# Sandwich block on one core: inverse roots of the feed-forward part's norms made on GpSimd by a bit guess and three Newton steps

## The reference

```
_layernorm(x) = (x - mean(x)) / sqrt(var(x) + 1e-5)        # over the last axis, 128
x = x + _layernorm(attention(_layernorm(x)))               # 16 heads of 8, relative bias, causal
x = x + _layernorm(ffn(_layernorm(x)))
ffn(x): h = silu(x @ w1.T * s1) * (x @ w2.T * s2)          # 128 -> 512
        h = gelu(h @ h1.T * sh1)                           # 512 -> 512
        h = gelu(h @ h2.T * sh2)                           # 512 -> 512
        return h @ w3.T * s3                               # 512 -> 128
```

## Time and profile before

| what | us |
|---|---|
| median of 3 runs | 781.52 |
| the profiled execution, whole | 783.46 |
| its span, first to last instruction | 781.7 |
| feed-forward stage, from the first matmul of layer 0 to the end | about 570 to 781.7 |
| ScalarE table loads at the roots of `stage3` (L1716, L1720) | 8 of 1.283 |
| `Sqrt` of `rs` in `stage3`, each | 0.208 |

### The profile page before, as it was taken

How to read it: one execution, slowest core, us unless ns; L and a number is a source line. 1 busy time by engine, 2 the same in 40 slices (tenths; PEclk the granted TensorE clock), 3 DMA queues, 4 the chain that set the end, 5 groups by cost and what they waited for, 6 DMA issues and landing times. The chain is left out here.

```text
span 781.7 us, 19102 instructions
## 1 busy us (share of the span) xinstructions
PE 648.1 (83%) x8066; PEld 471.8 (60%) x8066; DVE 551.1 (70%) x928; ACT 557.1 (71%) x654; POOL 273.9 (35%) x185
## 2 busy tenths in 40 slices
PE   4527743499999999999999999997779899898993
PEld 2213313367667667676676766764568688687682
DVE  3829983277777778778787777876665757768546
ACT  1445542389798798988989889887657867778663
POOL 2213341806309045090450813601062181441801
PEclk9777875589999999999999999998989999999998
DMA  3471376122314214123142231404020000000001
GB/s 72 114 268 56 100 216 188 18 62 58 101 32 95 64 52 114 55 75 83 44 114 63 66 93 35 123 29 136 14 81 2 0 1 1 1 27 2 1 27 55
DMA packets 40143, 53.53 MB, mean 68 GB/s; under 512 B 5664, under 2 KB 30528, under 8 KB 37632
## 3 DMA queue, kind: packets, MB, share of 16 engines
q1 hardware_dynamic: 40056, 52.28, 24.6%
HBM read 39.59 MB, written 11.94 MB: 66 GB/s over the span
## 5 line engine op out<-in xcount | busy, mean ns | idle before, releaser
L961 PE MATMUL p_s<-q_sb,k_sb 96*128 96x128 bf16 (+1 forms) x1600 | 171.0, 249 | 18.3 <-DVE probs L1107 14.5
L1225 ACT ACTIVATE probs<-p_s 128x1024 f32<-128x1024 f32 x160 | 156.6, 1017 | 18.2 <-DVE p_s L1116 10.6
L1225 ACT ACTIVATE probs<-probs 128x1024 f32<-128x1024 f32 x128 | 133.5, 1055 | 46.4 <-DVE probs L1107 46.2
L1005 PE MATMUL p_o<-probs,v_sb 128*32 128x128 f32 (+1 forms) x3200 | 159.8, 331 | 7.5 <-ACT o_acc L1243 4.7
L961 PEld LDWEIGHTS p_s<-q_sb,k_sb 96*128 96x128 bf16 x1600 | 113.0, 100 | 77.6 <-issue 29.4
L917 POOL TENSOR_SCALAR_AFFINE_SELECT even_b<-even_b 128x2048 f32<-128x2048 f32 x32 | 75.4, 2357 | 220.2 <-ACT even_b L1236 220.2
L1107 DVE TENSOR_TENSOR probs<-p_s,even_b 128x1024 f32<-128x1024 f32 x96 | 115.0, 1220 | 27.5 <-PE p_s L961 15.4
L1005 PEld LDWEIGHTS p_o<-probs,v_sb 128*32 128x32 f32 x3200 | 84.6, 111 | 40.7 <-issue 13.5
L1654 PE MATMUL p_z<-hid_hi,h_hi 128*128 128x512 f32 x256 | 102.0, 398 | 1.7 <-POOL hid_lo L1575 1.7
L1657 PE MATMUL p_z<-hid_lo,h_hi 128*128 128x512 f32 x256 | 101.0, 395 | 0.0
L982 PE MATMUL p_s<-q_rows,rel_w 72*128 72x64 bf16 x2048 | 84.8, 197 | 18.2 <-DVE probs L1107 8.7
(11 more groups left out here) (177 smaller groups left out, 883.7 us busy)
## 6 DMA issues: line engine op xcount, KB each, us to landing
k_sb<-k_dram SPq DMA_DIRECT2D x48, 192.0 KB
q_sb<-q_dram SPq DMA_DIRECT2D x16, 576.0 KB
q_rows<-qr_dram SPq DMA_DIRECT2D x42, 192.0 KB
q_dram<-q_parts SPq DMA_DIRECT2D x12, 256.0 KB, 6.1
k_dram<-k_parts SPq DMA_DIRECT2D x12, 256.0 KB, 6.1
qr_dram<-q_turned SPq DMA_DIRECT2D x12, 256.0 KB, 6.1
x_all<-in_L_attn_x_dram SPq DMA_DIRECT2D x4, 512.0 KB, 4.7
every<-in_L_ffn_h_w_dram SPq DMA_DIRECT2D x2, 1024.0 KB, 8.2
```

Of the source, the lines that this page charges most:

```text
L961: last = nc.tensor.matmul(slot[:, c:c + n * BLK], k_sb[hg][:, h * S + j * BLK:h * S + (j + 1) * BLK], ap(q_sb[hg], at, [[HG * S, KROWS], [ ...
L1005: last = nc.tensor.matmul(p_o[32 * h:32 * h + 32, at:at + blocks * BLK], v_sb[hg][:, j, h * 32:(h + 1) * 32], probs[n % PBUFS][:, h, col * ...
L1225: nc.scalar.activation(to, got, ACT.Exp, scale=SCALE).then_inc(t_exp, 1)
```

## The change

In `stage3` the roots go from ScalarE to GpSimd. There `inverse_root` makes 1 / sqrt(x) of the 128 by 8 tile in 13 instructions (`ROOT_OPS`), each of which waits for the one before: a first guess from the bits (one), and then three Newton steps of four. Two columns of the statistics tile (`st3` or `st4`, stride of 6 elements) are its working space, and the result is in column 1. VectorE's reciprocals in `stage3` go as well. GpSimd's order becomes: `pre_root(n+1, 0)`, `gather(n+2)`, `add_x(n+1)`, `post_root(n-1)`, `pre_root(n+1, 1)`, the splits, `add_x1(n-1)`, and at the end `post_root(3)`. The norms of batch 0 in the attention stage keep `Sqrt` and reciprocal.

```diff
--- before.py
+++ after.py
@@ -86,6 +86,9 @@
 NZ = 4
 HC = HID // 128
 PRE, POST = 12, 5
+ROOT_GUESS = 0x5F3759DF
+ROOT_STEPS = 3
+ROOT_OPS = 1 + 4 * ROOT_STEPS
 
 
 class First:
@@ -127,9 +130,33 @@
     nc.vector.tensor_scalar(rs[:, :], mv[:, :, 1], EPS, None, ALU.add).then_inc(chain, 1)
 
 
+def inverse_root(nc, pool, x, room, done, at):
+
+    bits = mybir.dt.int32
+    t, y = room[:, :, 0], room[:, :, 1]
+    nc.gpsimd.tensor_scalar(y.bitcast(bits), x[:, :].bitcast(bits), -0.5, float(ROOT_GUESS), ALU.mult,
+                            ALU.add).then_inc(done, 1)
+    for i in range(ROOT_STEPS):
+        pool.wait_ge(done, at + 1 + 4 * i)
+        nc.gpsimd.tensor_tensor(t, y, y, ALU.mult).then_inc(done, 1)
+        pool.wait_ge(done, at + 2 + 4 * i)
+        nc.gpsimd.tensor_tensor(t, t, x[:, :], ALU.mult).then_inc(done, 1)
+        pool.wait_ge(done, at + 3 + 4 * i)
+        nc.gpsimd.tensor_scalar(t, t, -0.5, 1.5, ALU.mult, ALU.add).then_inc(done, 1)
+        pool.wait_ge(done, at + 4 + 4 * i)
+        nc.gpsimd.tensor_tensor(y, y, t, ALU.mult).then_inc(done, 1)
+
+
 def normalised(nc, dve, ffn, n, which, src):
 
     at = n * PRE + 6 + 5 * which
+    if n > 0:
+        dve.wait_ge(ffn.r_root, (2 * n + which - 1) * ROOT_OPS)
+        for t in range(NB):
+            last = nc.vector.tensor_scalar(ffn.y[:, t, :], src[:, t, :], ffn.mv[:, t, 0:1], ffn.st[:, t, 1:2],
+                                           ALU.subtract, ALU.mult)
+        last.then_inc(ffn.r_dv, 2)
+        return
     dve.wait_ge(ffn.r_sd, n * 2 + which + 1)
     nc.vector.reciprocal(ffn.rs[:, :], ffn.rs[:, :]).then_inc(ffn.r_dv, 1)
     dve.wait_ge(ffn.r_dv, at)
@@ -758,6 +785,7 @@
     ffn.r_x, ffn.r_otr, ffn.r_oT, ffn.r_y, ffn.r_dv = (sem(n) for n in ("r_x", "r_otr", "r_oT", "r_y", "r_dv"))
     ffn.r_sd, ffn.r_x1, ffn.r_xtr, ffn.r_hi, ffn.r_lo = (sem(n) for n in ("r_sd", "r_x1", "r_xtr", "r_hi", "r_lo"))
     ffn.r_oc = sem("r_oc")
+    ffn.r_root = sem("r_root")
 
 
 
@@ -1453,7 +1481,7 @@
     f_mul = sem("f_mul")
     f_hi, f_lo0 = sem("f_hi"), sem("f_lo0")
     f_ghi, f_lo = sem("f_ghi"), sem("f_lo")
-    w_zT, w_tr, w_dv, w_sd, w_sum, w_last = (sem(n) for n in ("w_zT", "w_tr", "w_dv", "w_sd", "w_sum", "w_last"))
+    w_zT, w_tr, w_dv, w_root, w_sum, w_last = (sem(n) for n in ("w_zT", "w_tr", "w_dv", "w_root", "w_sum", "w_last"))
     w_out = [sem(f"w_out{p}") for p in range(2)]
 
     def layer_tiles(n, l, k):
@@ -1575,18 +1603,33 @@
                     nc.gpsimd.tensor_tensor(hid_lo[k][0][:, o, :], act_f[k][:, o, :], hid_hi[k][0][:, o, :].bitcast(F32),
                                             ALU.subtract).then_inc(f_lo0, 1)
 
+            def pre_root(n, which):
+                pool.wait_ge(r_dv, n * PRE + (5, 10)[which])
+                inverse_root(nc, pool, ffn.rs, ffn.st, ffn.r_root, (2 * n + which - 2) * ROOT_OPS)
+
+            def post_root(n):
+                pool.wait_ge(w_dv, n * POST + 3)
+                inverse_root(nc, pool, rs4, st4, w_root, n * ROOT_OPS)
+
             gather(1)
             for k in range(NC):
                 split(0, k)
             for n in range(B):
+                if n + 1 < B:
+                    pre_root(n + 1, 0)
                 if n + 2 < B:
                     gather(n + 2)
                 if n + 1 < B:
                     add_x(n + 1)
+                if n > 0:
+                    post_root(n - 1)
+                if n + 1 < B:
+                    pre_root(n + 1, 1)
                     for k in range(NC):
                         split(n + 1, k)
                 if n > 0:
                     add_x1(n - 1)
+            post_root(B - 1)
 
         @block.tensor
         def _(pe):
@@ -1711,14 +1754,6 @@
                     act.wait_ge(r_otr, n * NC + k + 1)
                     nc.scalar.activation(oT[:, k * FC:(k + 1) * FC], p_pre[k][:, :], ACT.Copy).then_inc(r_oT, 1)
 
-            def pre_root(n, which):
-                act.wait_ge(r_dv, n * PRE + (5, 10)[which])
-                nc.scalar.activation(ffn.rs[:, :], ffn.rs[:, :], ACT.Sqrt).then_inc(r_sd, 1)
-
-            def post_root(n):
-                act.wait_ge(w_dv, n * POST + 3)
-                nc.scalar.activation(rs4[:, :], rs4[:, :], ACT.Sqrt).then_inc(w_sd, 1)
-
             def pre_hi(n):
                 if n > 0:
                     act.wait_ge(f_z, Z[n - 1, 0, 1, 1, HC - 1])
@@ -1773,13 +1808,7 @@
                     weight_hi(4)
                 gelus(n, 1, 0)
                 gelus(n, 1, 1)
-                if n + 1 < B:
-                    pre_root(n + 1, 0)
                 gelus(n, 2, 0)
-                if n > 0:
-                    post_root(n - 1)
-                if n + 1 < B:
-                    pre_root(n + 1, 1)
                 gelus(n, 2, 1)
                 if n + 1 < B:
                     pre_hi(n + 1)
@@ -1789,7 +1818,6 @@
                 outputs(n, 1)
                 if n + 1 < B:
                     silus(n + 1, 1)
-            post_root(B - 1)
 
         @block.vector
         def _(dve):
@@ -1826,15 +1854,13 @@
                            w_dv, n * POST + 1, ffn.alone)
 
             def post_out(n):
-                dve.wait_ge(w_sd, n + 1)
-                nc.vector.reciprocal(rs4[:, :], rs4[:, :]).then_inc(w_dv, 1)
-                dve.wait_ge(w_dv, n * POST + 4)
+                dve.wait_ge(w_root, (n + 1) * ROOT_OPS)
                 if n > 1:
                     dve.wait_ge(w_out[n % 2], (n // 2) * 16)
                 for t in range(NB):
                     last = nc.vector.tensor_scalar(res[n % 2][:, t, :], p_post[t // NT][:, (t % NT) * 128:(t % NT + 1) * 128],
-                                                   mv4[:, t, 0:1], rs4[:, t:t + 1], ALU.subtract, ALU.mult)
-                last.then_inc(w_dv, 1)
+                                                   mv4[:, t, 0:1], st4[:, t, 1:2], ALU.subtract, ALU.mult)
+                last.then_inc(w_dv, 2)
 
             def weight_lo(g):
                 dve.wait_ge(ffn.hi, EARLY + 1 + g + 1)
```

## The result

The changed kernel takes 793.44 us (median of 4 runs, 791.68 to 794.5) against 781.45 for the kernel before (4 runs): a ratio of 1.0156, 95% interval 1.0128 to 1.0183. By the ratio that is 12.2 us (the medians differ by 12.0), slower as forecast and inside the range (784 to 796), but 4 us more than the 7.9 of the sum. The profiled execution is the fastest of the four. Its span of 789.9 us is only 8.2 over that of the kernel before, and what it lacks is the subject of the experiments.

The account below looks back on a forecast made before the run. The prediction took the chain to `x1T_lo` in three turns and the last norm to set the end. Second roots 4.6 plus last root 3.3 made 7.9 us, on a median of 781.52: 789.4, range 784.0 to 796.0.

Parts of the forecast that it names:

- the sum: Whole change: 4.6 us for the second roots in three turns plus 3.3 for the last root, 7.9 us slower.
- the bare roots: Three second roots and the last, where nothing hides the root's time: 4.6 and 3.3 us slower.
- the clock: Rival: TensorE, idle over 3 us before the transposes, drops to 1.2 GHz; at most 4.4 us more, 793.8; chance 0.07.
- R: Time of one inverse root on GpSimd, thirteen dependent instructions: 3.9 us, with ends of 2.3 and 6.8.
- First and output roots hidden: First roots fit in 5.4 us of cover in turn 0; output roots hidden, 5 us free in turns 1 and 2.
- VectorE's risk: Sign of being wrong: VectorE's splits of (n,2,0), 2.60 us for four, grow longer beside GpSimd's steps, delaying second statistics.
- one of the signs: Prediction is wrong if the first or the output roots show up as waits of VectorE.
- Second roots: From `rs` to the normalising in turns 0 to 2: 0.51 us becomes 4.06, 3.55 more a turn.
- The gain behind them: From normalising to TensorE's start, 7.16 us becomes 5.5, giving back 1.66; a dropped reciprocal gives 0.24 in turns 1 and 2.
- the cover of 1.1 us in turns 1 and 2: In the clock rival, 1.1 us of TensorE's delay is covered by its wait for VectorE's products.
- The last root: Last norm after turn 3, fully bare: 3.55 us more less 0.24 for a reciprocal, 3.3 slower.
- No slack behind: All that hangs on `x1T_lo` moves with it; no slack seen in the next turn to take up the delay.

Follow-up runs that it names:

- the second run of the changed kernel: The changed kernel measured and profiled once more, with nothing altered: 794.74 us, ratio 1.016 to the kernel before.
- the run with TensorE kept busy: Changed kernel plus 12 matmuls with unused results in each of turns 0 to 2, in TensorE's idle time ahead of the transposes: 787.78 us, ratio 1.0078.
- The run of the last root alone: The kernel before with only the last root moved to GpSimd: ratio 1.0034.
- the one-step kernel: Changed kernel with one Newton step instead of three in the roots, less accurate: 778.57 us, ratio 0.9949.
- the best one: First and output roots on GpSimd, second on VectorE, last on ScalarE, plus an early small SiLU and a moved last normalising: 774.18 us, ratio 0.9904.
- critical roots on VectorE: Changed kernel with the three second roots and the last root on VectorE, two Newton steps, nine instructions: 781.4 us, ratio 0.9987.
- the two best versions: First and output roots on GpSimd, second on VectorE, last on ScalarE: 777.11 us; with early SiLU and moved normalising too: 774.18 us.
- hidden roots alone: The kernel before with only the six first and output roots on GpSimd, three Newton steps: ratio 0.9991.

## Why the prediction was right, and where it was not

The forecast was slower by 7.9; it is 12.2 to 12.5. The direction and the bare roots were right, and the range held because it was wide enough for the clock, to which the prediction had given a chance of 0.07. From the second run of the changed kernel against the kernel before, the 12.2 us between the spans are: the first statistics of turn 0 come 0.4 sooner; from there to the second ones it is 0.5 less; the second roots cost 3.3 + 3.35 + 3.5; the stretches behind them change by +1.0, -0.8 and +0.1; from the first product of turn 0 to the first statistics of turn 1 it is 0.75 less; the late first root of turn 2 costs 0.3; it is 0.3 less ahead of the last norm, and the last root costs 3.3.

- **R.** Right. Forecast 4.06 with its handoffs, measured 3.82 to 4.01. The fixed parts from long instructions came out a little high for two inputs (0.25, measured 0.21) and low for one (0.19).
- **First and output roots hidden.** Right in the time (0.9991), not in the margin. A root of 3.9 was set against 5.4 us of cover, but beside the splits it took 5.3, since four of its thirteen steps grew by 0.4. The prediction had named this contention only as VectorE's risk; beside the splits it was GpSimd that was slowed. And the cover was read in turn 0 alone: in turn 2 of the kernel before VectorE is back 3.5 us behind the statistics (ready at 698.24, last split done at 701.77), and there even a root of 3.9 does not fit. In the changed kernel VectorE waits 1.86 for it, which is one of the signs that the prediction named for being wrong, and the second statistics come 0.3 to 0.6 later. The row of the kernel before, with 0.83 of waiting for ScalarE's root:

```profile
702.60 0.20 DVE L134 RECIPROCAL rs<-rs 128x8 f32<-128x8 f32 x1 [0.83 <-ACT rs L1716]
```

- **Second roots.** The price is right (3.55 forecast, 3.3 to 3.5 measured). The gain behind them, 1.66, and 1.9 with the reciprocal, is near what was measured at full clock: 9.42 - 7.99 = 1.4 in turn 0 and 10.4 - 8.2 = 2.2 in the others.
- **The clock.** This is the step that failed, in its chance and in one term. It stood there as a rival with 0.07 and up to 4.4 us, 793.8; the median is 793.44. That the two agree so well is partly chance: at full clock the change cost 6.1 (the run with TensorE kept busy) where the sum had 7.9, and the clock cost another 6.1 where the rival had at most 4.4. The sum had no term for the 0.75 us behind turn 0 and took the gains behind the second roots of turns 1 and 2 some 0.3 too small each.

Set against the same stretches at full clock the clock took 10.41 - 7.99 = 2.4, 9.63 - 8.22 = 1.4 and 10.48 - 8.22 = 2.3, 6.1 us in all, and the run with TensorE kept busy gave back 6. The argument against it was that in turn 1 an idle time of 2.0 us had left the clock alone. But the change made idle times of over 3, and the same 2.0 had been enough for a slow stretch in two turns of the kernel before, in turn 0 and in turn 2, which the prediction did not look at:

```profile
720.40:724.40 4.00, 3.98 (x10) 0.58 0.00 0
```

The term that failed is the cover of 1.1 us in turns 1 and 2: at full clock ScalarE's way (transposes, a layer, output, table load of 1.28, SiLU) comes to the first product 8.0 behind the start of the normalising (turn 0) and VectorE's, with the last normalising of the batch before, 8.2, so only 0.2 is covered and what slows TensorE shows at once. The sum followed `x1T_lo` alone and did not walk ScalarE's way.

- **One thing was given back.** The 0.75 us behind turn 0 are two things. The slow stretch behind the old wait for `x1T_lo` is gone. And `gather`, which the change put behind the first root, no longer runs beside a split of turn 1. The run of the last root alone tells them apart: there the stretch behind the wait in turn 0 is at full clock, `gather` has its old place, and the distance is 22.97 us, against 23.18 before and 22.41 changed. So the clock alone would give 0.2 back, since the split then falls beside `gather`:

```profile
640.84 1.50 POOL L1619 COPY o_cur<-vo_all 128x1024 f32<-128x1024 f32 x1
```

```profile
641.65 1.24 DVE L1959 TENSOR_TENSOR hid_lo<-act_f,hid_hi 128x512 fp32r<-128x512 f32 x1 [0.20 <-ACT hid_hi L1841]
```

In the changed kernel the same split takes 0.69. In its new place `gather` lengthens VectorE's first normalising instead, from 2.14 to 2.81 us in turns 0 and 1. That stays hidden: from the first to the second statistics it is 15.4 and 16.2 us, against 15.9 and 16.2 before.

- **The last root.** 3.3 forecast. Its wait grew by 3.3 and the run of it alone gave 2.7 (1.7 to 3.6).
- **No slack behind.** Right: the terms above, taken one for one, add up to the difference of the spans, and those of the one-step kernel and the best one nearly do.

## What to carry to other kernels

Thirteen dependent steps on a tiny tile cost thirteen times the fixed part and the gap. On GpSimd that was 3.8 us, where ScalarE with VectorE's reciprocal needed 0.5 and VectorE alone 1.5, with two Newton steps in place of three. Relieving an engine that is not late pays only if the replacement is shorter than the wait that it ends: here the move cost 12 us with GpSimd's root in the bare places. It gained 5 with the second roots on VectorE and the last left on ScalarE, and 7.5 once the table load and a normalising had gone from the freed stretch. When a change makes TensorE idle ahead of work on the critical chain, price that work at the lower clock as well, and give it a real chance. And read the cover of a hidden step in every turn, not in one.

## What the runs showed of the hardware

GpSimd's smallest arithmetic instruction took 0.21 us, one input or two, with 0.08 to the next one that waits for it. Beside VectorE's instructions single ones took 0.51 to 0.76, while VectorE's splits in the same stretch kept their 0.69. Beside longer instructions of GpSimd it was VectorE that was slowed: a split took 1.24 us beside the copy of 1.50, and one of 2.52 stands beside an addition of 2.83 in the kernel before (turn 2, 691.85). VectorE's small instructions took 0.17 to 0.18 with 0.04 between, the same for two operations in one as for one.

Idle times of TensorE up to 1.65 us ahead of the transposes had no slow stretch behind them in any of twelve turns (one step, critical roots on VectorE, and the two best versions, with 0.84), nor in the run with TensorE kept busy. Of the nine idle times of 2.0 us ahead of `x1T_lo` (kernel before, hidden roots alone, last root alone) five had a granted clock of 0.51 to 0.65 in the 3.5 or 4 us behind them and four had 1.00. Of the twelve of 3.2 to 4.0 us ten had transposes of 1.63 to 1.97 us. In turn 2 of the first profile they took 1.09 and the clock fell behind them: it is 0.66 in the mean over 4 us from 721.7. So the first profile, with one turn spared and another slowed late, is 2 us under the median.
